# Five products a tile are added to their neighbours by an accumulating DMA from tile 8 on; GpSimd then adds four instead of seven, and TensorE sums twelve instead of fourteen

## The chip, the cores and the metric

The kernel runs on one core of a Trainium2 chip. It has five engines that run their own instruction queues and wait for each other by semaphores: TensorE (PE, with its weight loads as PEld), VectorE (DVE), ScalarE (ACT), GpSimd (POOL) and SyncE (SP), which here only issues DMAs. The metric is the time of one execution on the device, in microseconds; of several, the median is shown.

## The reference

A block of two halves on an image of 4 x 128 channels x 56 x 56. The first half is an involution: a 7 x 7 convolution whose kernel is computed for each pixel and each of 16 groups of channels. The second is a mixture of experts (8 experts, the best 2 for each token, hidden width 341).

```python
# conv half, on the layer-normed x
h = einsum('bchw,oc->bohw', xk, reduce_w) + reduce_b
kern = einsum('bchw,oc->bohw', h, span_w) + span_b      # 49 taps x 16 groups a pixel
out = (kern * patches).sum(axis=3)                      # sum over the 49 taps
x = x + out
# ffn half, on tokens
t = t + sum over the 2 chosen experts of gate * (silu(h1) * h3) @ w2.T
```

The change concerns only how `(kern * patches).sum` adds up its 49 products.

## The kernel before

The image is cut into 28 tiles of 8 rows (448 pixels). The 49 taps of a tile are taken as 24 pairs and one single, so 25 products (`TAPS`), numbered u = 0 to 24; a product of a pair is 128 x 896 floats, its two halves are two taps. One step of the program is one product: step S belongs to tile `p` and place `j` with `S = 25 p + j`, and each engine's program is written out as a loop over all steps (`for S in range(FIRST, END)`), so that each engine's order is fixed when the kernel is built.

For product g = 25 t + u:

- TensorE computes the pixel-wise kernel of the pair into `kern_ps[g % 2]` (`span_unit`, L586; two matmuls, one for the single). It waits until product g - 2 is done, since there are two such buffers.
- VectorE multiplies it with the shifted window of the normed image and writes `prod[g % 8]` (`unit`, L851; L839 for the single). The ring `prod` has `PRING = 8` slots, so before it writes, VectorE waits until the product eight before has been used (`consumer`).
- A product is then added up in one of three ways. **GpSimd** adds it to `acc_p` (`add`, L1084 for the first two, L1088 for the others). **VectorE** folds it into the next product: that product is made in `kern_ps` (L845) and the one before is added (L848). **TensorE** sums it into `acc_ps` by eight transposing matmuls with the identity (`sum_unit`, L601), the last of which for a tile takes `acc_p`.

Before, for tiles from `LATE = 8` on, GpSimd takes products 0, 3, 6, ..., 21 (seven additions), VectorE folds 10, 13, 16 and 19 into 11, 14, 17 and 20, and TensorE sums the other 13 and `acc_p`: 14 sums. The steps at which TensorE does its sums come from a small planner at the top of the kernel (`SUM_AT`): a sum is put two steps after its product or later, at the first step whose estimated load is under 1.3, and five steps after at the latest.

```python
while _left and at(_t, _left[0]) + 2 <= _S and (LOAD.get(_S, 0) < 1.3
        or min(at(_t, _left[0]) + 5, at(_t + 1, 2)) <= _S):
    SUM_AT.setdefault(_S, []).append((_t, _left.pop(0)))
```

When the tile is summed, VectorE adds the residual (`x1`, L1053), and ScalarE and GpSimd do its layer norm (`rsqrt`: L1074 and L1076 on GpSimd, for both norms). Tokens are routed to experts in groups of two tiles; GpSimd scatters their rows to DRAM by indirect DMAs (`scatter`, L1097), and the expert blocks of 512 tokens are computed on TensorE in between (L623 to L627, L536; `hid` on VectorE, L1024). Their results are added to the output by accumulating indirect DMAs (`add_rows`, L1109). Scatters stand at nine places of a late tile (`SCATTER_J`), token additions at nine (`ADD_J`). GpSimd's order within a step is: `rsqrt`, `add`, `scatter`, `add_rows`. After the last product the remaining expert blocks run as a tail.

Of the kernel before, what the change touches and what calls it, by code (L numbers as in the profile page):

```python
# [9 lines left out]
ALU = mybir.AluOpType  # L10
# [31 lines left out]
LATE = 8  # L42
BY_POOL = [tuple(range(0, 21, 2)) if t < LATE else tuple(range(0, 22, 3)) for t in range(TILES)]
BY_DVE = [() if t < LATE else (10, 13, 16, 19) for t in range(TILES)]
BY_PE = [tuple(u for u in range(TAPS) if u not in BY_POOL[t] + BY_DVE[t]) for t in range(TILES)]
ADD0 = [sum(len(BY_POOL[i]) - 1 for i in range(t)) for t in range(TILES + 1)]
PRING = 8
# [167 lines left out]
for _t in range(TILES):  # L215
    _S = at(_t, J_X1 + 1)
    _left = list(BY_PE[_t])
    while _left:
        while _left and at(_t, _left[0]) + 2 <= _S and (LOAD.get(_S, 0) < 1.3 or min(at(_t, _left[0]) + 5, at(_t + 1, 2)) <= _S):
            SUM_AT.setdefault(_S, []).append((_t, _left.pop(0)))  # L220
            LOAD[_S] = LOAD.get(_S, 0) + 1.04
        _S += 1
# [15 lines left out]
def build(nc, x, w_red, b_red, w_span, router, w13, w2, ident, lower, consts, tabs, ids, empty, out):  # L238
    with ExitStack() as ctx:  # L239
# [108 lines left out]
        s_prod = sem("s_prod")  # L348
        s_inner = sem("s_inner")
        s_sum = sem("s_sum")  # L350
        s_padd = sem("s_padd")
# [61 lines left out]
        def token_rows(dram, t):  # L413
            return dram[t * N:(t + 1) * N, :].rearrange("(q p) c -> p q c", p=SUB)

        def consumer(eng, t, u):

            if u in BY_POOL[t]:
                eng.wait_ge(s_padd, ADD0[t] + max(BY_POOL[t].index(u), 1))
            elif u in BY_DVE[t]:  # L420
                eng.wait_ge(s_prod, t * TAPS + u + 2)
            else:
                eng.wait_ge(s_sum, SUM_NO[(t, u)])
# [99 lines left out]
        def _(pe):  # L523
# [65 lines left out]
            def sum_unit(t, u):  # L589
                if u == BY_PE[t][0] and t:  # L590
                    pe.wait_ge(s_x1, t)
                if u < TAPS:
                    pe.wait_ge(s_prod, t * TAPS + u + 1)
                    src = prod[:, (t * TAPS + u) % PRING, :]
                else:
                    pe.wait_ge(s_padd, ADD0[t + 1])
                    src = acc_p[:]
# [463 lines left out]
        def _(pool):  # L1061
# [16 lines left out]
            def add(t, k):  # L1078
# [7 lines left out]
                else:  # L1086
                    pool.wait_ge(s_padd, ADD0[t] + k - 1)
                    g_.tensor_tensor(acc_p[:], acc_p[:], prod[:, (t * TAPS + u) % PRING, :], ALU.add).then_inc(s_padd, 1)  # L1088

            def scatter(t, q, k):  # L1090
                n = t * SUBS + q
# [21 lines left out]
            for S in range(FIRST, END):  # L1113
# [5 lines left out]
                if 0 <= p < TILES and j in BY_POOL[p][1:]:  # L1119
                    add(p, BY_POOL[p].index(j))  # L1120
                if S in SCATTER_AT:
                    scatter(*SCATTER_AT[S])
# [60 lines left out]
```

## Time and profile before

| | |
|---|---|
| median of 3 runs | 1502.02 us (1501.6 to 1506.93) |
| the profiled execution | 1498.94 us, span 1497.1 us |
| busy in the span | PE 1243.9 (83%), DVE 1122.8 (75%), POOL 1112.2 (74%), ACT 579.5 (39%) us |
| granted TensorE clock, mean | 0.95 |
| DMA | 120.40 MB, mean 80 GB/s |

Busy time of an engine counts its instructions and not its waiting. The average over the span mixes two stages: in the first, to about 1203 us, products are made; the tail after it has expert blocks only. A wait is put down to whatever came last before the waiting instruction began.

### The profile page before, as it was taken

To read this page: it belongs to the slowest core of one execution; us is meant where nothing else is said; L and a number is where in the kernel's file an instruction comes from. 1 tells how busy PE (TensorE), PEld (TensorE's weight loads), DVE (VectorE), ACT (ScalarE), POOL (GpSimd) and SP (SyncE) were. 2 spreads that over 40 slices of the span, in tenths; PEclk is the share of its full clock that TensorE was granted. 3 is DMA by queue.
4 is the path that set the end of the run, shared out by engine and by line. 5 is a ranking of instruction groups with operands and counts; after the bars stand their busy time and mean duration, and the time that the engine had idled before them with its cause. 6 is when DMAs were issued, how large, how long until landed. Compare 5 with 4: busy or idle time off the path is not lost. (4 is left out here: it accounts for less than half of the span.)

```text
span 1497.1 us, 23125 instructions
## 1 busy us (share of the span) xinstructions
PE 1243.9 (83%) x7667; PEld 1015.6 (68%) x7667; DVE 1122.8 (75%) x1663; ACT 579.5 (39%) x1960; POOL 1112.2 (74%) x788
## 2 busy tenths in 40 slices
PE   4898878788988989899899898899989887587771
PEld 2676767676766777677787777777778676465661
DVE  5998888988898998888889898888889943222220
ACT  4333333334443444444345343454434244133230
POOL 4787979784686887678788687877778875665665
PEclk9999898998999999999999999999999999899996
DMA  4111111112232242332324232243322445666652
GB/s 124 41 60 48 59 49 59 49 31 88 53 79 60 69 97 63 88 78 60 85 59 103 62 86 62 60 100 83 71 58 48 105 119 129 174 137 134 145 117 25
DMA packets 93346, 120.40 MB, mean 80 GB/s; under 512 B 11531, under 2 KB 72428, under 8 KB 93082
## 3 DMA queue, kind: packets, MB, share of 16 engines
q1 hardware_dynamic: 53802, 90.97, 20.0%
q0 software_dynamic: 39424, 27.96, 13.3%
q8 instruction: 61, 1.00, 0.3%
q14 instruction: 59, 0.48, 0.1%
HBM read 78.92 MB, written 42.65 MB: 81 GB/s over the span
## 5 line engine op out<-in xcount | busy, mean ns | idle before, releaser
L851 DVE TENSOR_TENSOR prod<-kern_ps,xn 128x896 f32<-128x896 f32 x592 | 627.9, 1082 | 65.7 <-PE kern_ps L586 63.2
L586 PE MATMUL kern_ps<-h_stack,span 98*128 98x448 f32 x1372 | 466.3, 426 | 112.7 <-DVE prod L851 72.1
L1088 POOL TENSOR_TENSOR acc_p<-acc_p,prod 128x896 f32<-128x896 f32 x192 | 435.9, 2270 | 74.1 <-DVE prod L851 69.4
L1109 POOL DMA_INDIRECT out<-y_tok,idx x224 | 351.6, 1570 | 137.4 <-issue 66.2
L601 PE MATMUL acc_ps<-ident_sb,prod 128*112 128x128 f32 x2864 | 388.4, 280 | 0.0
L601 PEld LDWEIGHTS acc_ps<-ident_sb,prod 128*112 128x112 f32 x2864 | 341.3, 137 | 37.9 <-DVE x L1053 7.8
L586 PEld LDWEIGHTS kern_ps<-h_stack,span 98*128 98x128 f32 x1372 | 227.1, 200 | 205.5 <-DVE prod L851 121.5
L1097 POOL DMA_INDIRECT xs<-rows_x,slots x224 | 219.0, 978 | 61.0 <-issue 41.3
L536 PEld LDWEIGHTS bank<-w2b,hid 114*128 114x128 f32 x1344 | 181.7, 202 | 50.7 <-DVE xf_lo L1046 26.0
L536 PE MATMUL bank<-w2b,hid 114*128 114x128 f32 x1344 | 190.1, 288 | 26.2 <-DVE xf_lo L1046 15.9
L780 ACT ACTIVATE silu<-h_ps 114x512 f32<-114x512 f32 x132 | 79.0, 598 | 235.0 <-PE h_ps L627 235.0
L1024 DVE TENSOR_TENSOR hid<-silu,h_ps 114x512 f32<-114x512 f32 x132 | 89.9, 681 | 97.9 <-ACT silu L780 68.8
L623 PE MATMUL h_ps<-xf_hi,wb 128*114 128x512 f32 x264 | 118.5, 449 | 15.3 <-ACT silu L780 13.6
L1084 POOL TENSOR_TENSOR acc_p<-prod 128x896 f32<-128x896 f32 x28 | 62.9, 2247 | 85.9 <-DVE prod L851 52.2
L685 ACT ACTIVATE y_tok<-bank,xb 128x128 f32<-128x128 f32 x224 | 64.1, 373 | 118.6 <-PE bank L536 98.1
L627 PE MATMUL h_ps<-xf_lo,wb 128*114 128x512 f32 x264 | 106.1, 402 | 0.0
L624 PE MATMUL h_ps<-xf_hi,wb 128*114 128x512 f32 x264 | 105.9, 401 | 0.0
L845 DVE TENSOR_TENSOR kern_ps<-kern_ps,xn 128x896 f32<-128x896 f32 x80 | 87.2, 1090 | 12.3 <-PE kern_ps L586 11.4
L848 DVE TENSOR_TENSOR prod<-kern_ps,prod 128x896 f32<-128x896 f32 x80 | 87.3, 1091 | 2.8
L1024 DVE TENSOR_TENSOR hid<-silu,kern_ps 114x512 f32<-114x512 f32 x36 | 24.7, 685 | 84.2 <-ACT silu L780 63.1
L1074 POOL TENSOR_TENSOR rstd_ln<-veps_ln,minus_half 112x4 f32<-112x4 f32 x56 | 67.0, 1196 | 15.0 <-ACT veps_ln L718 14.9
L755 ACT ACTIVATE rows_x<-x,shift_ln,rstd_ln 112x128 f32<-112x128 f32 x112 | 47.8, 485 | 56.4 <-POOL shift_ln L1076 56.3
(154 smaller groups left out, 1349.9 us busy)
## 6 DMA issues: line engine op xcount, KB each, us to landing
wb<-wexp SPq DMA_DIRECT2D x56, 684.0 KB, 5.4
xb<-xs SPq DMA_DIRECT2D x56, 264.0 KB, 3.0
w2b<-in_w SPq DMA_DIRECT2D x56, 171.0 KB
xt<-in_x SPq DMA_DIRECT2D x28, 224.0 KB, 3.4
out<-x SPq DMA_DIRECT2D x28, 224.0 KB, 2.6
wexp<-wb SPq DMA_DIRECT2D x8, 684.0 KB, 3.2
xs<-rows_x,slots POOLq DMA_INDIRECT x224, 2.3
out<-y_tok,idx POOLq DMA_INDIRECT x224
```

The lines of the kernel that those rows point to most:

```text
L536: i = mm(bank[:, k * C:(k + 1) * C], hid[:, (CPE * b + c) % HR, k * 128:(k + 1) * 128], w2b[:, b % 2, c, :], start=c == 0 and k == 0, stop ...
L586: last = mm(kern_ps[:, g % 2, i, 0:N], span[:, k * C:(k + 1) * C], h_stack[:, t % 2, :], start=True, stop=True)
L601: last = mm(acc_ps[0:SUB, k * C:(k + 1) * C], src[:, at_:at_ + SUB], ident_sb[:], is_transpose=True, start=u == BY_PE[t][0] and i == 0 and ...
L623: mm(ps, lo, xf_hi[:, b % 2, :], start=True, stop=False)
L624: mm(ps, hi, xf_hi[:, b % 2, :], start=False, stop=False)
L627: mm(ps, hi, xf_lo[:, b % 2, :], start=False, stop=True).then_inc(done, 1)
L848: v.tensor_tensor(dst.rearrange("p (i n) -> p i n", i=2), kern, prod[:, (g - 1) % PRING, :].rearrange("p (i n) -> p i n", i=2), ALU.add).t ...
L851: v.tensor_tensor(pair_rows(dst), kern.rearrange("p i (r w) -> p i r w", w=W), taps, ALU.mult).then_inc(s_prod, 1)
L1024: v.tensor_tensor(hid[:, n % HR, :], silu[:, n % 2, :], h_at(n, 1), ALU.mult).then_inc(s_hid, 1)
L1088: g_.tensor_tensor(acc_p[:], acc_p[:], prod[:, (t * TAPS + u) % PRING, :], ALU.add).then_inc(s_padd, 1)
L1097: g_.indirect_dma_start(out=xs, out_offset=bass.IndirectOffsetOnAxis(ap=slots[:, k, n:n + 1], axis=0), in_=rows_x[:, t % XN2RING, q, k, :] ...
L1109: g_.indirect_dma_start(out=out, out_offset=bass.IndirectOffsetOnAxis(ap=idx[:, b % XBRING, q:q + 1], axis=0), in_=y_tok[:, b % 2, q * C:( ...
```

## The change

From tile 8 on five products (1, 5, 11, 17 and 22, `BY_DMA`) are added to their right neighbours (2, 6, 12, 18 and 23) in SBUF by a DMA that accumulates, issued from GpSimd at the step of the neighbour, after GpSimd's own addition of that step and before its scatter. It waits for the neighbour's product. Four semaphores in turn (`MRING`) tell of the landings. GpSimd's own products are now 0, 4, 8, 15 and 21 (four additions), VectorE's folds are the same four, and TensorE sums eleven products and `acc_p`. A sum of a merged neighbour waits for the merge, and the planner puts it five steps after its product or later (`soonest`); `BY_PE` is sorted by the earliest step. VectorE, before it takes the slot of a merged product again, waits for that merge.

```diff
-BY_POOL = [tuple(range(0, 21, 2)) if t < LATE else tuple(range(0, 22, 3)) for t in range(TILES)]
+BY_POOL = [tuple(range(0, 21, 2)) if t < LATE else (0, 4, 8, 15, 21) for t in range(TILES)]
 BY_DVE = [() if t < LATE else (10, 13, 16, 19) for t in range(TILES)]
-BY_PE = [tuple(u for u in range(TAPS) if u not in BY_POOL[t] + BY_DVE[t]) for t in range(TILES)]
+
+BY_DMA = [() if t < LATE else (1, 5, 11, 17, 22) for t in range(TILES)]
+MERGE_NO = {(t, u): n for n, (t, u) in enumerate((t, u) for t in range(TILES) for u in BY_DMA[t])}
+MRING = 4
+
+def soonest(t, u):
+
+    return 5 if u - 1 in BY_DMA[t] else 2
+
+BY_PE = [tuple(sorted((u for u in range(TAPS) if u not in BY_POOL[t] + BY_DVE[t] + BY_DMA[t]),
+                      key=lambda u: u + soonest(t, u))) for t in range(TILES)]
...
-        while _left and at(_t, _left[0]) + 2 <= _S and (LOAD.get(_S, 0) < 1.3 or min(at(_t, _left[0]) + 5, at(_t + 1, 2)) <= _S):
+        while _left and at(_t, _left[0]) + soonest(_t, _left[0]) <= _S and (LOAD.get(_S, 0) < 1.3 or min(at(_t, _left[0]) + 5, at(_t + 1, 2)) <= _S):
...
+        def merged(eng, t, u):
+
+            n = MERGE_NO[(t, u)]
+            eng.wait_ge(s_merge[n % MRING], 16 * (n // MRING + 1))
+
         def consumer(eng, t, u):
 
             if u in BY_POOL[t]:
                 eng.wait_ge(s_padd, ADD0[t] + max(BY_POOL[t].index(u), 1))
+            elif u in BY_DMA[t]:
+                merged(eng, t, u)
...
                     pe.wait_ge(s_prod, t * TAPS + u + 1)
+                    if u - 1 in BY_DMA[t]:
+                        merged(pe, t, u - 1)
...
+            def merge(t, u):
+
+                n = MERGE_NO[(t, u)]
+                g = t * TAPS + u
+                pool.wait_ge(s_prod, g + 2)
+                if n >= MRING:
+                    pool.wait_ge(s_merge[n % MRING], 16 * (n // MRING))
+                g_.dma_start(prod[:, (g + 1) % PRING, :], prod[:, g % PRING, :], accum_op=ALU.add).then_inc(s_merge[n % MRING], 16)
...
+                if 0 <= p < TILES and j - 1 in BY_DMA[p]:
+                    merge(p, j - 1)
```

The program's order shows what stands where. On GpSimd, in tile 20 from step 4 to step 12, stood before (L1088 the additions of products 6, 9 and 12; L1097 a scatter, L1109 a token addition, L1074 and L1076 the second norm's `rsqrt`):

```order
L1097 DMA xs<-rows_x,slots 104960x132
L1109 DMA out<-y_tok,idx 13056x128
L1088 TENSOR_TENSOR acc_p<-acc_p,prod 128x896
L1097 DMA xs<-rows_x,slots 104960x132
L1109 DMA out<-y_tok,idx 13056x128
L1074 TENSOR_TENSOR rstd_ln<-veps_ln,minus_half 112x4
L1076 TENSOR_TENSOR shift_ln<-negmean_ln,rstd_ln 112x4
L1088 TENSOR_TENSOR acc_p<-acc_p,prod 128x896
L1097 DMA xs<-rows_x,slots 104960x132
L1109 DMA out<-y_tok,idx 13056x128
L1088 TENSOR_TENSOR acc_p<-acc_p,prod 128x896
```

and stands now, after the `rsqrt` of step 4 (L1106 and L1110 the additions of products 4 and 8, L1119 the merges of 5 and of 11, L1128 a scatter, L1140 a token addition):

```order
L1106 TENSOR_TENSOR acc_p<-prod 128x896
L1128 DMA xs<-rows_x,slots 104960x132
L1140 DMA out<-y_tok,idx 13056x128
L1119 DMA prod<-prod 128x896
L1128 DMA xs<-rows_x,slots 104960x132
L1110 TENSOR_TENSOR acc_p<-acc_p,prod 128x896
L1140 DMA out<-y_tok,idx 13056x128
L1096 TENSOR_TENSOR rstd_ln<-veps_ln,minus_half 112x4
L1098 TENSOR_TENSOR shift_ln<-negmean_ln,rstd_ln 112x4
L1128 DMA xs<-rows_x,slots 104960x132
L1140 DMA out<-y_tok,idx 13056x128
L1119 DMA prod<-prod 128x896
```

The merge of 5 into 6 stands behind the addition of product 4, a scatter and a token addition; five instructions stand between it and the merge of 11 into 12, besides the small ones of the norm.

On TensorE, in tile 20 from step 9 to step 12, stood before (L586 the matmuls of a product's kernel, L601 a sum, L623 to L627 an expert slot, L548 transposes of the next tile's input):

```order
L586 MATMUL kern_ps<-h_stack,span 128x448 x2
L601 MATMUL acc_ps<-ident_sb,prod 112x128 x8
L548 MATMUL bank<-ident_sb,xn_tok 128x112 x4
L586 MATMUL kern_ps<-h_stack,span 128x448 x2
L601 MATMUL acc_ps<-ident_sb,prod 112x128 x8
L623 MATMUL h_ps<-xf_hi,wb 114x512
L624 MATMUL h_ps<-xf_hi,wb 114x512
L627 MATMUL h_ps<-xf_lo,wb 114x512
L586 MATMUL kern_ps<-h_stack,span 128x448 x2
L601 MATMUL acc_ps<-ident_sb,prod 112x128 x8
L586 MATMUL kern_ps<-h_stack,span 128x448 x2
```

and stands now (L606, L623, L645 to L649 and L568 are the same in the new numbering):

```order
L606 MATMUL kern_ps<-h_stack,span 128x448 x2
L623 MATMUL acc_ps<-ident_sb,prod 112x128 x8
L568 MATMUL bank<-ident_sb,xn_tok 128x112 x4
L606 MATMUL kern_ps<-h_stack,span 128x448 x2
L645 MATMUL h_ps<-xf_hi,wb 114x512
L646 MATMUL h_ps<-xf_hi,wb 114x512
L649 MATMUL h_ps<-xf_lo,wb 114x512
L606 MATMUL kern_ps<-h_stack,span 128x448 x2
L623 MATMUL acc_ps<-ident_sb,prod 112x128 x8
L606 MATMUL kern_ps<-h_stack,span 128x448 x2
```

The sum of step 10 is gone, and the one of step 11 is now that of product 6, which waits for the merge of 5; the kernel matmuls of step 12 stand behind it.

## Rows read from the trace of the kernel before

**Rows 1.** Windows: busy us (count) by engine, clock, DMA share, GB/s.
```profile
347.00:1203.20 856.20, 766.61 (x4851) 638.00 (x4851) 749.87 (x1123) 359.37 (x1224) 668.86 (x481) 0.97 0.32 73
1203.20:1497.00 293.80, 200.55 (x1169) 156.18 (x1167) 77.67 (x172) 93.51 (x253) 181.48 (x128) 0.92 0.56 125
```

**Rows 2.** Chain of waits in the tail: start us, us, what.
```profile
1355.68 1.55 POOL out L1109
...
1357.53 3.95 DMA out<-y_tok,idx
...
1362.45 1.55 POOL out L1109
```

**Rows 3.** Waits, 347 to 1203 us: total us, times, longest.
```profile
PE kern_ps L586 <- DVE prod L851: 38.8, 53, 2.7
...
PE kern_ps L586 <- DVE prod L848: 33.5, 43, 1.6
DVE prod L851 <- PE kern_ps L586: 32.9, 58, 1.5
...
DVE kern_ps L845 <- PE kern_ps L586: 11.0, 14, 1.3
DVE hid L1024 <- PE h_ps L627: 10.7, 17, 2.0
...
DVE kern_ps L908 <- PE kern_ps L586: 8.2, 9, 1.8
```

**Rows 4.** TensorE by line, 346 to 1203 us: busy us, mean ns | idle.
```profile
L601 PE MATMUL acc_ps<-ident_sb,prod 128*112 128x128 f32 x1891 | 251.2, 276 | 0.0
```

**Rows 5.** GpSimd by line and shape, 346 to 1203 us.
```profile
L1088 POOL TENSOR_TENSOR acc_p<-acc_p,prod 128x896 f32<-128x896 f32 x114 | 270.7, 2375 | 61.7 <-DVE prod L851 61.5
L1109 POOL DMA_INDIRECT out<-y_tok,idx x124 | 196.1, 1582 | 44.8 <-issue 34.6 <-ACT y_tok L685 6.8 <-DMA out<-y_tok,idx 2.1
L1097 POOL DMA_INDIRECT xs<-rows_x,slots x150 | 146.0, 973 | 34.9 <-issue 19.9 <-POOL acc_p L1088 12.0 <-ACT rows_x L740 2.3
L1074 POOL TENSOR_TENSOR rstd_ln<-veps_ln,minus_half 112x4 f32<-112x4 f32 x37 | 46.6, 1259 | 8.7 <-ACT veps_ln L718 8.7
```

**Rows 6.** The page: DMA queues (packets, MB, share); issues with landing.
```profile
q1 hardware_dynamic: 53802, 90.97, 20.0%
q0 software_dynamic: 39424, 27.96, 13.3%
...
wb<-wexp SPq DMA_DIRECT2D x56, 684.0 KB, 5.4
...
xs<-rows_x,slots POOLq DMA_INDIRECT x224, 2.3
```

**Rows 7.** Timeline of tile 20, VectorE: start us, us, instruction.
```profile
851.52 1.09 DVE L851 TENSOR_TENSOR prod<-kern_ps,xn 128x896 f32<-128x896 f32 x1 [0.56 <-PE kern_ps L586]
...
853.12 4.22 DVE L851 TENSOR_TENSOR prod<-kern_ps,xn 128x896 f32<-128x896 f32 x4
...
864.05 1.08 DVE L851 TENSOR_TENSOR prod<-kern_ps,xn 128x896 f32<-128x896 f32 x1
```

**Rows 8.** Timeline of tile 20, TensorE.
```profile
861.29 0.57 PE L586 MATMUL kern_ps<-h_stack,span 98*128 98x448 f32 x2
861.71 1.04 PE L601 MATMUL acc_ps<-ident_sb,prod 128*112 128x128 f32 x8
...
870.81 0.65 PE L586 MATMUL kern_ps<-h_stack,span 98*128 98x448 f32 x2
```

**Rows 9.** Timeline of tile 20, GpSimd.
```profile
852.51 1.04 POOL L1074 TENSOR_TENSOR rstd_ln<-veps_ln,minus_half 112x4 f32<-112x4 f32 x1 [0.59 <-ACT veps_ln L718]
853.63 0.20 POOL L1076 TENSOR_TENSOR shift_ln<-negmean_ln,rstd_ln 112x4 f32<-112x4 f32 x1
...
868.47 2.70 POOL L1088 TENSOR_TENSOR acc_p<-acc_p,prod 128x896 f32<-128x896 f32 x1
```

More of the change, by code:

```diff
@@ L349, in build @@
         s_inner = sem("s_inner")
+        s_merge = [sem(f"s_merge{i}") for i in range(MRING)]
         s_sum = sem("s_sum")
```

## The prediction

> **What bounds the kernel now.** I read the windows first. [rows 1] splits the span: from 347 to 1203 us run 19 of the 20 changed tiles, and from 1203 to 1497 us comes a tail in which no product is made any more. In the first stretch TensorE is busy 767 of 856 us, VectorE 750, GpSimd 669, and the 16 DMA engines 0.32 of the time. Three engines are nearly full and the transfers are not. The chain of waits comes next: in the tail it is made of the token additions alone, GpSimd's issues and their landings [rows 2]. No product, no sum and no addition to `acc_p` stands in it, so the change cannot touch the tail; what the first stretch gains or loses shifts the tail one for one.
>
> Within the stretch the waits [rows 3] say how TensorE and VectorE hold each other. `kern_ps` has two buffers, so TensorE may be one product ahead and no more. VectorE waits for TensorE's `kern_ps` 32.9 us before plain products, 11.0 before folded ones and 8.2 before routing steps that stand in front of a product, and 10.7 us for the hidden layer: 62.8 us, or 3.3 us a tile. TensorE in turn waits 38.8 + 33.5 = 72.3 us for VectorE's products, 3.8 us a tile. So neither is the bound alone: work taken from TensorE helps only in those steps where VectorE was the one waiting, and a new wait of TensorE hurts at once only where TensorE had no time to spare.
>
> **What is removed.** Two sums a tile leave TensorE. The sums of products are 1891 matmuls in 251.2 us [rows 4], eight to a sum, hence 1.06 us a sum; 2 x 1.06 x 20 tiles = 43 us of TensorE. Both ends of what that is worth: nothing if VectorE sets the pace in those steps, all 43 us if TensorE does. The waits are split about evenly between the two (62.8 against 72.3 us), so I take half, 21 us. The second order fence shows one of the places: step 10 loses its sum, in a run of steps in which TensorE did not idle.
>
> GpSimd loses three additions a tile, each 270.7 / 114 = 2.37 us [rows 5]: 7.1 us a tile. It gets five issues of an accumulating DMA. No such issue from one tile to another stands in the trace. The nearest rows are the scatter (112 rows, 0.97 us) and the token addition, which accumulates (128 rows, 1.58 us) [rows 5]; I take 1.3 us, between them, and keep both ends. 5 x (1.3 + 0.16 between instructions) = 7.3 us. So GpSimd stays as full as it was (669 of 856 us), and this is the point on which the rest turns: the merges stand in a queue that is not early.
>
> VectorE's own work does not change: the same 25 products and the same four folds. Where it takes a slot of `prod` again it now waits for a merge instead of an addition or a sum. That wait comes eight products after the source, about 10 us after the merge may begin, and I cost it at nothing as long as a merge lands within that; with the late ends below it would begin to bind at step 13 or 19, but behind the same merge that TensorE already waits for, so it isn't added.
>
> **What a merge takes.** It moves 128 x 3584 B = 459 KB. From its issue, a scatter of 56 KB lands in 2.3 us (a median), a load of 684 KB of weights in 5.4 us [rows 6]. Over the whole profile the hardware queue q1 moved 90.97 MB in 20.0% of 16 x 1497 us, 19.0 GB/s an engine; the software queue q0, in which the accumulating transfers run, 27.96 MB in 13.3%, 8.8 GB/s [rows 6]. A merge gives each of 16 engines 28.7 KB: 1.5 us at the one rate and 3.3 us at the other. Low end of landing: 2.3 + 1.5 = 3.8 us. High end: the token addition of the tail, issued at 1355.68 and landed at 1357.53 + 3.95 = 1361.48 [rows 2], takes 5.8 us from its issue for only 64 KB, in DRAM; with 3.3 - 0.4 us more of data 8.7 us. A merge reads and writes SBUF like the scatter's source and needs no reading of DRAM, so I stay nearer to the scatter: 2.3 + 0.3 for a longer issue + 2.1 of data more than the scatter's + 0.5 for sharing the engines with the loads = 5.2 us. (100 merges x 2.3 us of every engine add 0.26 to the DMA share of 0.32: no saturation.)
>
> The Trainium skill ("DMA: Bandwidth & Descriptors", the section on the anatomy of one DMA from GpSimd) gives about 2.0 us plus the bytes at 436 GB/s; an estimate from that page is 3.1 us for a merge. The trace agrees for the small scatter and not for the 684 KB load, which takes 5.4 us where the page's line gives 3.6. The skill's "Collectives: The Full Stack" (the bandwidth ceiling: the fold count) says that an adding transfer has two sources to read and so runs at half the rate of a copy; q0 at 8.8 against q1 at 19.0 GB/s fits that, though small rows are in it too.
>
> **When a merge is asked for.** I follow tile 20, in its own times. The planner puts the sum that needs the merge of 5 into 6 on TensorE in step 11, and that of 11 into 12 in step 17. Before, product 4 ends at 852.61, product 6 near 855.2 (the second of the four that start at 853.12), product 12 at 865.13 [rows 7]. TensorE has finished the kernel matmuls of step 11 at 861.86 and of step 17 at 871.46 [rows 8]; there it would stop.
>
> GpSimd's queue (the first order fence) before the merge of 5: the little products for `rstd` and `shift`, which end at 853.83 [rows 9], then the first addition (2.37), a scatter (0.98 + 0.16) and a token addition (1.58 + 0.30): 859.2. Product 6 has been ready for 4.0 us by then. It lands at 859.2 + 5.2 = 864.4, that is 2.5 us after TensorE stands at it. Then, in the queue: the merge's issue 1.46, scatter 1.14, addition 2.37, token addition 1.88, `rstd` and `shift` 1.55, scatter 1.14, token addition 1.88: the merge of 11 goes out at 870.6 and lands at 875.8, 4.3 us after TensorE came to it before the change, of which 2.5 have been lost already. That GpSimd is this late is no fiction of mine: the trace of before has its addition of product 12 start at 868.47 [rows 9], 3.3 us after that product.
>
> Tile 20 is a full one. There were 124 token additions and 150 scatters in 19 tiles [rows 5], 6.5 and 7.9 a tile where nine places for each are planned, so 0.28 and 0.12 of the places are empty. Up to step 17 three of each stand in the queue: 3 x (0.28 x 1.88 + 0.12 x 1.14) = 2.0 us less on average. 4.3 - 2.0 = 2.3 us a tile; some of it falls into time in which TensorE waited for VectorE anyway (folded products stand at steps 11, 14, 17 and 20), so I take 1.9. The merges of 17, 22 and 1 are issued when GpSimd has caught up, and their products leave five steps of about 1.8 us: 9 us less the step or so by which TensorE runs ahead, against 5.2: nothing. Sum: 1.9 x 20 = 38 us lost.
>
> What stands behind the waiting sum on TensorE is the kernel matmul of step 12 (second order fence), and VectorE's product 12 waits for that: the stall reaches the pace with little in between.
>
> **The sum.** -21 + 38 = +17 us. The profiled execution took 1498.9 us with a span of 1497.1; the median of the runs shown is 1502.0, 3.1 above it, and I set the difference on the median: 1519 us.
>
> **The rivals.**
> First, the merges land soon enough, and the kernel is faster. Place: TensorE at the sums of steps 11 and 17. With the low ends, landing 3.8 and issue 0.97, the queue reaches the merge of 11 at 870.3 and it lands at 874.1, 2.6 us after TensorE, less 2.0 for empty places: 0.6 us x 20 = 12 us, against 21 of relief: 1493 us; with more of the 43 us given back, down to 1480. The point from which it decides: a loss of 21 us is 1.05 us a tile, 0.85 less than mine, so a landing below about 4.3 us from the issue makes the kernel faster. For it: the scatter's 2.3 us, and half-idle DMA engines. Against: 4.0 us of lateness on GpSimd before the transfer even begins. By the Trainium skill's line for one DMA, above, the landing would be under this point.
>
> Second, no change. TensorE idles 3.8 us a tile for VectorE [rows 3]; if the merges' stalls fall into that, and what is saved at TensorE goes there too, the stretch stays at VectorE's pace: 1502 us. For it: VectorE is busy 750 of 856 us and its work is untouched. Against: VectorE has 3.3 us a tile of waiting for TensorE.
>
> Third, the transfer is slow, near its high end. With issue 1.58 and landing 8.7, 870.9 + 8.7 - 871.5 - 2.0 = 6.1 us a tile, 122 us, less 21: 1603 us. VectorE's wait for a slot would join in. Half-way, at 7 us, it is 3.7 x 20 - 21 = 53: 1555 us. For it: the token additions' 5.8 us. Against: these go to DRAM.
>
> **How the numbers follow.** The forecast, a few microseconds lost to late merges net of the relief, has 0.42; the first rival 0.28; the second 0.20; the third 0.10. About 0.5%, 7.5 us, is what a measurement of this kernel can tell from no change (the three runs lie between 1501.6 and 1506.9). Faster: the first rival, 0.28; same: 0.20; slower: 0.42 + 0.10 = 0.52. The forecast's own range is 1510 to 1540. Eight in ten takes in most of the first rival and the third to a landing of about 7 us: 1484 to 1560.
>
> **What would show it.** Right: the issue-to-landing of the merges near 5 us; the merge of 5 issued some 3 to 4 us after product 6; a new row among the waits, TensorE's sums for the merge, of 1 us and more a piece at steps 11 and 17; VectorE's waits for `kern_ps` grown there and shrunk in the steps around the tile's start; GpSimd as busy as before; the tail 294 us long. The forecast is wrong if the landing is 4 us or less, if an issue on GpSimd costs well under 1 us (its queue would then never be late), or if the rows of waits for the merge are short and the changed tiles take less than the 45.1 us they take now (856.2 / 19).

## The result and the profile after

The changed kernel takes 1555.2 us (median of 4 runs, 1549.1 to 1560.4) against 1501.8 (4 runs): ratio 1.0345, 95% interval 1.0319 to 1.037, so 3.5% slower, 53 us. The profiled execution took 1556.3 us with a span of 1554.5, which is 57.4 above the span of before. One run of the kernel before, in the last group of runs below, took 6467 us and is left out of its median.

Where the time went is answered first by the windows. Here are, of the changed kernel, the same 19 tiles as in [rows 1] and the tail after them, in the same columns (us, busy us and count of TensorE, its weight load, VectorE, ScalarE, GpSimd, then the granted clock, the DMA share and GB/s):

```profile
347.50:1256.60 909.10, 758.54 (x4558) 620.59 (x4558) 746.77 (x1124) 357.90 (x1224) 643.62 (x519) 0.94 0.56 118
1256.60:1554.00 297.40, 203.24 (x1162) 159.21 (x1160) 77.51 (x170) 94.32 (x253) 182.21 (x129) 0.89 0.58 124
```

The stretch of 19 tiles takes 909.1 us where it took 856.2: 52.9 of the 57.4 us, or 2.8 us a tile. The tail has grown by 4, the start by half a microsecond. No engine has become fuller: TensorE is busy 759 us (767 before), VectorE 747 (750), GpSimd 644 (669). All stand longer. Only the DMA share is much higher, 0.56 for 0.32.

The waits of the same stretch say what they stand for (total us, times, longest); compare [rows 3]:

```profile
PE acc_ps L623 <- DMA prod<-prod: 67.2, 39, 6.0
PE kern_ps L606 <- DVE prod L870: 30.1, 29, 1.7
PE kern_ps L606 <- DVE prod L873: 25.3, 48, 1.3
...
PE bank L574 <- ACT rows_x L777: 1.6, 3, 0.7
DVE prod L873 <- PE kern_ps L606: 42.6, 48, 5.3
DVE xf_lo L1068 <- ACT xf_hi L699: 19.6, 17, 5.2
DVE ge L1000 <- PE kern_ps L606: 17.9, 4, 6.5
DVE hid L1046 <- PE h_ps L649: 17.5, 15, 2.7
...
DVE kern_ps L930 <- PE kern_ps L606: 8.4, 8, 1.8
DVE kern_ps L867 <- PE kern_ps L606: 5.8, 14, 1.3
```

The first row is new: TensorE stands at a sum until a merge has landed, 67 us. Its waits for VectorE shrank only from 72.3 to 55.4 us. VectorE waits more for TensorE: the longest piece before a plain product is 5.3 us where it was 1.5, the mark of a TensorE that has stopped. Over the whole span the page has the same wait at 68.8 us, in the group that answers to [rows 4], and the merge's issues stand further down:

```profile
L623 PE MATMUL acc_ps<-ident_sb,prod 128*112 128x128 f32 x2544 | 359.4, 287 | 73.8 <-DMA prod<-prod 68.8
...
L1119 POOL DMA_DIRECT2D prod<-prod x100 | 114.2, 1142 | 101.9 <-DVE prod L873 101.0
```

GpSimd by line in the stretch answers to [rows 5]:

```profile
L1140 POOL DMA_INDIRECT out<-y_tok,idx x124 | 197.3, 1591 | 34.8 <-issue 34.6 <-ACT rows_x L762 0.2
L1128 POOL DMA_INDIRECT xs<-rows_x,slots x150 | 149.9, 1000 | 40.9 <-issue 33.6 <-ACT rows_x L762 5.7 <-POOL acc_p L1106 1.0
L1110 POOL TENSOR_TENSOR acc_p<-acc_p,prod 128x896 f32<-128x896 f32 x57 | 123.7, 2169 | 66.9 <-DVE prod L873 66.6
L1119 POOL DMA_DIRECT2D prod<-prod x95 | 109.4, 1152 | 97.8 <-DVE prod L873 96.9 <-DVE prod L861 0.8
```

95 issues in 19 tiles, 1.15 us each on average. GpSimd also idles 97 us in front of them, waiting for the product, 46 times of 95: about half of the merges are not late at all when they are issued. The page's queues answer to [rows 6]:

```profile
q0 software_dynamic: 53824, 73.84, 28.9%
q1 hardware_dynamic: 53802, 90.97, 19.7%
```

The merges brought q0 45.9 MB in 14,400 packets; its share rose from 13.3% of 1497 us to 28.9% of 1554.5.

Now the walk through tile 20, which answers to [rows 7 to 9]. GpSimd's timeline (start us, us, instruction, idle before it) around the merge of 5:

```profile
881.46 2.10 POOL L1106 TENSOR_TENSOR acc_p<-prod 128x896 f32<-128x896 f32 x1
883.73 1.03 POOL L1128 DMA_INDIRECT xs<-rows_x,slots  x1 [0.16 <-POOL acc_p L1106]
885.06 1.61 POOL L1140 DMA_INDIRECT out<-y_tok,idx  x1 [0.30 <-issue]
886.08 1.57 POOL L1119 DMA_DIRECT2D prod<-prod  x1
...
896.69 1.54 POOL L1119 DMA_DIRECT2D prod<-prod  x1
```

VectorE's products 5 to 7 of the tile:

```profile
880.78 3.17 DVE L873 TENSOR_TENSOR prod<-kern_ps,xn 128x896 f32<-128x896 f32 x3
```

and TensorE at the sums of steps 11 and 17:

```profile
887.45 0.57 PE L606 MATMUL kern_ps<-h_stack,span 98*128 98x448 f32 x2
891.16 1.06 PE L623 MATMUL acc_ps<-ident_sb,prod 128*112 128x128 f32 x8 [3.14 <-DMA prod<-prod]
...
901.86 1.06 PE L623 MATMUL acc_ps<-ident_sb,prod 128*112 128x128 f32 x8 [0.39 <-DMA prod<-prod]
```

Product 6, the second of the three, is ready at 882.9. GpSimd comes to the merge at 886.1, 3.2 us later. TensorE is done with the kernel matmuls at 888.0 and starts the sum at 891.2: 5.1 us from the issue to the sum, 3.1 us stood. The merge of 11 is issued at 896.69 and its sum starts at 901.86, 5.2 us later, with 0.4 us stood. This tile follows the prediction's walk closely at step 11. The odd tile before it does not. SyncE's and GpSimd's issues in tile 19:

```profile
829.07 0.34 SPq L505 DMA_DIRECT2D xb<-xs  x1
829.46 0.42 SPq L530 DMA_DIRECT2D out<-x  x1
829.93 0.48 SPq L532 DMA_DIRECT2D xt<-in_x  x1
...
831.16 1.56 POOL L1119 DMA_DIRECT2D prod<-prod  x1
831.39 0.22 SPq L514 DMA_DIRECT2D wb<-wexp  x1
```

and its sum on TensorE:

```profile
841.44 1.93 PE L623 MATMUL acc_ps<-ident_sb,prod 128*112 128x128 f32 x8 [4.88 <-DMA prod<-prod]
```

Here the merge is asked for promptly, but 10.3 us pass from the issue to the sum, beside 264 + 224 + 224 + 684 KB of loads and stores, and TensorE stands 4.9 us. What I counted from the timeline over all 20 tiles, by merge: at that of 5 TensorE stands 46.1 us (in every tile), at that of 22 14.0, at that of 11 7.8, at that of 1 5.9, at that of 17 nothing: together the 73.8 us that the page shows as idle before these matmuls, of which it puts 68.8 on the merge.

The 46.1 us at the merge of 5 have two causes, and they go by the tile's number. In the ten even tiles (21.8 us) the merge goes out 1.2 to 4.5 us after product 6 and its sum starts 4.5 to 5.3 us after the issue. In the ten odd tiles (24.3 us) it goes out 0.3 to 1.6 us after the product, so GpSimd is hardly late, but 5.9 to 10.3 us pass from the issue to the sum. Those ten part again by the loads beside them. In tiles 11, 15, 19, 23 and 27 SyncE issues a load of expert weights (684 KB) within 3 us of the merge, and it takes 8.1 to 10.3 us; in the other five no such load is that near, and it takes 5.9 to 7.1 us.

### The profile page after: what moved, and what is told of

Read it like the earlier page. It is cut to its first block and busy times, and to the rows that moved or that the text cites. A ratio compares the mean times of both kernels' runs of the same rounds, so it can differ in the third digit from the quotient of the medians.

```text
span 1554.5 us, 22661 instructions
## 1 busy us (share of the span) xinstructions
PE 1237.2 (80%) x7347; PEld 998.3 (64%) x7347; DVE 1118.3 (72%) x1663; ACT 578.9 (37%) x1960; POOL 1086.5 (70%) x828
## 3 DMA queue, kind: packets, MB, share of 16 engines
q0 software_dynamic: 53824, 73.84, 28.9%
q1 hardware_dynamic: 53802, 90.97, 19.7%
## 5 line engine op out<-in xcount | busy, mean ns | idle before, releaser
L606 PE MATMUL kern_ps<-h_stack,span 98*128 98x448 f32 x1372 | 468.3, 427 | 97.7 <-DVE prod L873 60.4
L1140 POOL DMA_INDIRECT out<-y_tok,idx x224 | 352.7, 1575 | 130.8 <-issue 62.7
L623 PE MATMUL acc_ps<-ident_sb,prod 128*112 128x128 f32 x2544 | 359.4, 287 | 73.8 <-DMA prod<-prod 68.8
L623 PEld LDWEIGHTS acc_ps<-ident_sb,prod 128*112 128x112 f32 x2544 | 311.5, 141 | 120.0 <-issue 45.2
L606 PEld LDWEIGHTS kern_ps<-h_stack,span 98*128 98x128 f32 x1372 | 228.8, 201 | 189.4 <-DVE prod L873 102.2
L1110 POOL TENSOR_TENSOR acc_p<-acc_p,prod 128x896 f32<-128x896 f32 x132 | 282.5, 2140 | 81.1 <-DVE prod L873 76.5
L1128 POOL DMA_INDIRECT xs<-rows_x,slots x224 | 223.4, 997 | 67.2 <-issue 55.7
L556 PEld LDWEIGHTS bank<-w2b,hid 114*128 114x128 f32 x1344 | 185.1, 205 | 50.0 <-DVE xf_lo L1068 24.1
L556 PE MATMUL bank<-w2b,hid 114*128 114x128 f32 x1344 | 193.5, 291 | 25.5 <-DVE xf_lo L1068 13.6
L1119 POOL DMA_DIRECT2D prod<-prod x100 | 114.2, 1142 | 101.9 <-DVE prod L873 101.0
L645 PE MATMUL h_ps<-xf_hi,wb 128*114 128x512 f32 x264 | 119.4, 452 | 14.5 <-ACT silu L802 13.4
L649 PE MATMUL h_ps<-xf_lo,wb 128*114 128x512 f32 x264 | 107.3, 406 | 0.0
L1106 POOL TENSOR_TENSOR acc_p<-prod 128x896 f32<-128x896 f32 x28 | 59.0, 2106 | 50.0 <-PE acc_ps L623 32.4
L1096 POOL TENSOR_TENSOR rstd_ln<-veps_ln,minus_half 112x4 f32<-112x4 f32 x56 | 74.5, 1330 | 25.4 <-ACT veps_ln L740 25.3
```

Of the source, the lines that this page charges most:

```text
L556: i = mm(bank[:, k * C:(k + 1) * C], hid[:, (CPE * b + c) % HR, k * 128:(k + 1) * 128], w2b[:, b % 2, c, :], start=c == 0 and k == 0, stop ...
L606: last = mm(kern_ps[:, g % 2, i, 0:N], span[:, k * C:(k + 1) * C], h_stack[:, t % 2, :], start=True, stop=True)
L623: last = mm(acc_ps[0:SUB, k * C:(k + 1) * C], src[:, at_:at_ + SUB], ident_sb[:], is_transpose=True, start=u == BY_PE[t][0] and i == 0 and ...
L645: mm(ps, lo, xf_hi[:, b % 2, :], start=True, stop=False)
L649: mm(ps, hi, xf_lo[:, b % 2, :], start=False, stop=True).then_inc(done, 1)
L1119: g_.dma_start(prod[:, (g + 1) % PRING, :], prod[:, g % PRING, :], accum_op=ALU.add).then_inc(s_merge[n % MRING], 16)
```

## The experiments

Every ratio is to the kernel before, run on the same chip in the same group; its median was 1503.2, 1503.1 and 1503.7 us in the three groups. Experiments 1, 2, 5 and 6 are of the first group, 3, 7, 8 and 9 of the second, 4, 10, 11 and 12 of the third. Waits quoted are of the stretch from 347 to 1257 us.

**1. No merges at all.** GpSimd issues none, nothing waits for one, five products a tile are left out of the output. The rest keeps its order.

```diff
-                merged(eng, t, u)
+                pass
...
-                    if u - 1 in BY_DMA[t]:
-                        merged(pe, t, u - 1)
...
-                if 0 <= p < TILES and j - 1 in BY_DMA[p]:
-                    merge(p, j - 1)
```

> The changed kernel's order with the five merges a tile left out altogether, issue, transfer and waits; products 1, 5, 11, 17 and 22 of the late tiles are then missing from the output. It shows what the lighter TensorE and GpSimd are worth by themselves. Theory A (the whole loss is TensorE standing at sums whose merge has not landed, and the relief is what I took, about 21 us): 1475 to 1485 us, near 1480. Rival B (nothing is relieved, VectorE sets the pace): 1500 us or a little more. Rival C (the planner's moved sums are themselves bad for the pace): above 1505 us even without merges.

Measured: 1480.4 us, ratio 0.986 (0.9836 to 0.9884). Two sums and three additions fewer a tile are worth 23 us together. That is near the prediction's 21, but the 21 were for TensorE's two sums alone: the three additions had been set against the five issues. How the 23 us divide between the two engines no run separates, so the agreement may be partly luck.

**2. Merges issued, nobody waits for them.** They add a product onto itself (the same bytes), and TensorE's wait is gone.

```diff
-                    if u - 1 in BY_DMA[t]:
-                        merged(pe, t, u - 1)
...
-                g_.dma_start(prod[:, (g + 1) % PRING, :], prod[:, g % PRING, :], accum_op=ALU.add)...
+                g_.dma_start(prod[:, g % PRING, :], prod[:, g % PRING, :], accum_op=ALU.add)...
```

> All five merges a tile are issued at their places and move the same bytes, but each adds its product to itself and TensorE's sums do not wait for it (only the reuse of the slot does); the five products are missing from the sums. Theory A (the wait at TensorE): within 5 us of the kernel without merges, 1475 to 1490 us, and no wait of TensorE on a transfer. Rival D (the traffic itself is the cost: it slows the loads of weights and tokens, or GpSimd's queue with five issues of 1.0 to 1.5 us is what holds the pace): 1520 us or more, most of the 53 us still there.

Measured: 1500.1 us (10 runs), ratio 0.9977 (0.9964 to 0.999). My own number was missed: issuing and moving the merges alone costs 19.7 us, and takes back nearly the whole relief. The wait for them is then worth 1555.2 - 1500.1 = 55 us (of two groups of runs, in which the kernel before lies 1.4 us apart). Where the 20 us may sit, the waits of this kernel show:

```profile
ACT rows_x L775 <- POOL shift_ln L1096: 89.3, 19, 7.0
PE bank L574 <- ACT rows_x L775: 35.0, 12, 5.0
```

ScalarE waits for GpSimd's `shift`, the end of the second norm's small products, and TensorE for the rows that ScalarE normalises with it. The same two waits in the kernel before, and then in experiment 1:

```profile
ACT rows_x L755 <- POOL shift_ln L1076: 28.4, 16, 3.8
PE bank L554 <- ACT rows_x L755: 3.9, 2, 3.5
```

```profile
ACT rows_x L775 <- POOL shift_ln L1096: 60.4, 19, 5.6
PE bank L574 <- ACT rows_x L775: 13.5, 6, 3.3
```

So the norm was late before any merge was issued. The first two order fences show what may have done it: the change moved an addition (now of product 8, in step 8) from behind the norm's small products of step 9, where that of product 9 stood, to ahead of them. The issue of the merge of 5 then comes on top. ScalarE's wait goes from 28 to 60 us with the additions moved and to 89 with the issues.

**3. The same with half the bytes** separates the issue from the traffic.

```diff
-                g_.dma_start(prod[:, g % PRING, :], prod[:, g % PRING, :], accum_op=ALU.add)...
+                g_.dma_start(prod[:, g % PRING, 0:N], prod[:, g % PRING, 0:N], accum_op=ALU.add)...
```

> As the kernel in which nobody waits for the merges (1500 us), with half of the bytes of each, 1792 B a row; same number of issues and of packets. The 20 us between it and the kernel without merges are either transfers in the way of other transfers (theory D: then about half of them go, 1490 us) or five issues a tile of 1.0 to 1.5 us on GpSimd, behind which the second norm's rsqrt stands and for that TensorE (theory F: 1497 to 1502 us, no change, and TensorE still waits about 35 us for ScalarE's normed rows).

Measured: 1499.8 us (10 runs), ratio 0.9978 (0.9964 to 0.9993), the same as with all bytes. The software queue's share fell from 29.9% to 22.5% of the engines, nearly half of what the merges had added, and nothing was won. So the 20 us are not the bytes. They are what stayed the same, the five issues in GpSimd's queue or the number of packets; experiment 4 bears on which.

**4. The norm first.** Experiment 2, with the addition of product 8 and the token addition of step 8 put behind the second norm's small products:

```diff
+                if LATE <= p < TILES and j == 9:
+                    add(p, 2)
...
+                hold = LATE <= p < TILES and j == 8
```

> As the kernel in which nobody waits for the merges (1500 us; 20 us above the one without merges), but GpSimd does the second norm's rsqrt before its addition of product 8 (and the token addition of step 8) instead of after them. Theory F (the five issues make GpSimd late for that rsqrt, ScalarE then norms the rows late, and TensorE waits 35 us for them): most of that wait goes, 1483 to 1490 us. Rival J (the 20 us sit elsewhere: in VectorE's waits for GpSimd's additions, in TensorE's other waits): 1497 to 1502 us.

Measured: 1487.5 us, ratio 0.989 (0.9866 to 0.9914). And the same two waits:

```profile
ACT rows_x L775 <- POOL shift_ln L1096: 36.8, 19, 3.4
PE bank L574 <- ACT rows_x L775: 4.5, 4, 2.8
```

The norm's lateness was worth 13 us of this kernel. GpSimd's work is the same here; only its order differs. Not all of the 13 need belong to the issues: the edit also takes away what the moved addition does, and TensorE's wait for the rows falls by 30.5 us, to under the 13.5 of experiment 1. The control, this order with no merges at all, was not run.

**5. Four merges, without that of 5**, the whole kernel otherwise (TensorE has a sum more).

```diff
-BY_DMA = [() if t < LATE else (1, 5, 11, 17, 22) for t in range(TILES)]
+BY_DMA = [() if t < LATE else (1, 11, 17, 22) for t in range(TILES)]
```

> A whole kernel: only 1, 11, 17 and 22 are merged; TensorE sums 5 and 6 itself, so thirteen sums a tile instead of twelve. The merge of 5 accounts for 46 of the 74 us that TensorE waits for merges. Theory A: those 46 us go, a sum of 1.06 us comes back in 20 tiles at half its weight (10 us): about 1519 us (1510 to 1528). Rival E (any merge hurts alike, the 53 us are spread over the five): 1545 us. If the wait only moves to the next merge, between the two.

Measured: 1535.1 us, ratio 1.0204 (1.0155 to 1.0253). Expected by my count was 1519. The wait for merges fell to this row:

```profile
PE acc_ps L623 <- DMA prod<-prod: 28.7, 18, 4.1
```

The merge of 5 is the dearest, but 20 us are won and not 46: with it gone, the wait at that of 22 grew from 14 to 21 us.

**6. The merge of 5 earlier**, ahead of the addition of product 4.

```diff
+                if LATE <= p < TILES and j == 6:
+                    add(p, 1)
```

> A whole kernel: GpSimd issues the merge of 5 before its addition of product 4 instead of after it; all else as in the changed kernel. Theory A1 (the merge of 5 is late because it is issued late): in the even tiles it is issued 2.1 to 4.5 us after its product and lands 5.1 us later, in the odd tiles 0.3 to 1.6 us after it and lands 6 to 10 us later beside a load of weights. An addition is 2.1 us, so the even tiles should win about 2 us each and the odd ones little: 10 x 2 + 10 x 0.5 = 25 us, 1530 us. Rival A2 (the landing alone matters): no change, 1550 to 1556 us.

Measured: 1558.6 us, ratio 1.0378 (1.0345 to 1.041). Neither expectation held. In the even tiles the merge did come sooner, by some 1.6 us; in the odd ones it had been prompt already. TensorE's wait for that of 5 fell from 46 to 5.4 us in both, and mostly because TensorE itself came later (8.7 us after product 6, median, for 5.8). It was held by a wait that I had overlooked:

```profile
DVE prod L873 <- POOL acc_p L1106: 49.2, 18, 5.5
PE acc_ps L623 <- DMA prod<-prod: 28.0, 23, 3.7
```

The first addition also frees the slot of product 0, which VectorE needs for product 8. The run says nothing against the mechanism; it says that this addition has a date of its own.

**7. Scatter and token addition of steps 4 and 5 held** until the merge of 5 is issued.

```diff
+                hold = LATE <= p < TILES and j in (4, 5)
+                for S_ in (S - 2, S - 1, S) if LATE <= p < TILES and j == 6 else () if hold else (S,):
```

> A whole kernel: in late tiles the scatter of step 4 and the token addition of step 5 are held back on GpSimd until the merge of 5 is issued in step 6; the additions of products stay where they are, so no slot of prod is freed later. Putting the addition of product 4 behind that merge had taken 40 us of TensorE's wait for the merge of 5 away and given 49 us of VectorE waiting for the slot of product 0 instead. Theory A1 (half of the lateness is GpSimd's queue): the merge of 5 goes out up to 3.0 us sooner in the even tiles, where TensorE waited 22 us for it, and hardly sooner in the odd ones: 15 to 20 us won, 1535 to 1540 us. Rival A2 (the landing beside the loads sets it in all tiles, since an earlier merge meets the step's other transfers): less than 8 us won.

Measured: 1552.2 us, ratio 1.0323 (1.0301 to 1.0345). That is 3 us won, the rival's number, but not for the rival's reason. Two rows show the exchange:

```profile
PE acc_ps L623 <- DMA prod<-prod: 50.6, 33, 4.2
PE bank L574 <- ACT rows_x L777: 22.4, 10, 4.3
```

The merge waits fell by 17 us (at that of 5 from 46 to 17 us, by 19 in even tiles and by 10 in odd ones), and the transposes of the normalised rows, 1.6 us late in the changed kernel, are 22.4 us late: what I had pushed back now stands between the merge and the norm.

**8. Less traffic beside the merge of 5.** Half of each block's expert weights is loaded (the other half is left out), and the store of `x` and the load of the next input stand at step 14 instead of step 6.

```diff
-                                 wexp[bass.ds(w * C, C), :]).then_inc(s_wb[b % 2], 16)
+                                 wexp[bass.ds(w * C, C), 0:2 * HALL]).then_inc(s_wb[b % 2], 16)
...
-                if j == J_X1 + 1 and 1 <= p <= TILES:
+                if j == 14 and 1 <= p <= TILES:
```

> The changed kernel with less traffic beside the merge of 5: of each block's 684 KB of weights only the first half is loaded (the other half keeps what is in the buffer, so the expert outputs are wrong), and the x1 store and xt load of step 6 are issued at step 14. Theory G (in the odd tiles the merge of 5 lands 6 to 10 us after its issue because 0.9 to 1.4 MB of other loads are in flight): it lands in 5 to 6 us there, the 25 us of waits in odd tiles fall to about 8, those for 1 and 22 by half (10 us): 1525 to 1532 us. Rival H (the landing does not depend on the loads): 1550 us or more.

Measured: 1517.6 us (6 runs), ratio 1.0094 (1.0064 to 1.0125): 38 us less than the changed kernel, more than I expected. The same merge of tile 19 as above, GpSimd and TensorE:

```profile
827.90 1.56 POOL L1119 DMA_DIRECT2D prod<-prod  x1
```

```profile
834.34 1.05 PE L623 MATMUL acc_ps<-ident_sb,prod 128*112 128x128 f32 x8 [1.07 <-DMA prod<-prod]
```

6.4 us for 10.3. Over the ten odd tiles the last packet of the merge of 5 ends 5.2 us after the issue, median, where it was 7.2; in the even ones it stays at 4.6. Not every odd tile gained: from issue to sum it is still 8.9 us in tile 11 (10.3) and 7.0 in tile 21 (6.7). The edit took away less than it says, too: by the trace the store of `x`, in most cases with the load, still goes out within about 3 us of the merge of 5 in half of the 20 tiles. In the odd tiles TensorE's wait at the merge of 5 fell from about 24 to 9.5 us in all; in the even ones it did not (21.8 to 25.3). TensorE's whole wait for merges is then 39.4 us, 28 less than in the stretch of the changed kernel. The remaining 10 us I did not separate: VectorE also waits less for the experts' rows (`xf_lo` 12.8 us for 19.6), and both halves of the edit act together.

**9. The sum that needs the merge of 5 two steps later** (step 13).

```diff
-    return 5 if u - 1 in BY_DMA[t] else 2
+    return (7 if u == 6 else 5) if u - 1 in BY_DMA[t] else 2
```

> A whole kernel: TensorE's sum of product 6 stands seven steps after its product, in step 13, instead of five. Transfers, issues and lateness stay. Theory A (each us of TensorE's stand at the merge of 5 costs a us of pace): two steps are 3.2 us, so of the 46 us about 8 remain: 1515 to 1520 us. Rival I (the stall only turns into VectorE waiting for the slot of product 6, which product 14 takes): 1540 us or more, with VectorE idle before product 14.

Measured: 1531.7 us, ratio 1.0176 (1.0141 to 1.0212). The wait at the merge of 5 went from 46 to 1.4 us, but 23 us were won. Two rows show what came instead:

```profile
PE acc_ps L623 <- DMA prod<-prod: 35.8, 26, 3.6
PE bank L574 <- ACT rows_x L777: 18.1, 8, 4.0
```

The wait at the merge of 11 rose from 7.8 to 12.6 us, and the norm is late again, which fits that a TensorE standing at step 11 had given GpSimd time to catch up.

**10. Both: the late sum, and the norm first** as in experiment 4.

> A whole kernel: all five merges, TensorE's sum of product 6 in step 13 (1532 us by itself, with the wait for the merge of 5 gone but 18 us of waits for the normed rows instead) and GpSimd's second rsqrt before its addition of product 8. Theories A and F together: the 18 us go, 1512 to 1518 us. If VectorE's pace is held by the merges of 1, 11 and 22 alone, 1525 to 1532 us.

Measured: 1553.7 us, ratio 1.0352 (1.032 to 1.0385), a plain miss of some 38 us.

```profile
PE acc_ps L623 <- DMA prod<-prod: 62.0, 30, 5.6
```

The wait for the normalised rows is gone, but what I put behind the norm stands in front of the merge of 11: TensorE waits 38.3 us at that one. GpSimd has three customers between steps 4 and 13 (merge of 5, norm, merge of 11), and whichever is served first makes another late.

**11. Three merges** (1, 11, 17) and 14 sums.

```diff
+BY_DMA = [() if t < LATE else (1, 11, 17) for t in range(TILES)]
```

> A whole kernel: only 1, 11 and 17 are merged, the three for which TensorE waited 5.9, 7.8 and 0 us; TensorE does 14 sums as before the change, GpSimd four additions and three issues instead of seven additions. Without the merge of 5 alone it was 1535 us. Theory A (the waits for 5 and 22 are the loss): 1535 less the 21 us that TensorE waited there for the merge of 22, plus a sum at half its weight (10 us), and fewer collisions: 1515 to 1525 us. Theory F (GpSimd's queue is what was filled up): three issues instead of five and no merge ahead of the second norm's rsqrt: 1500 to 1510 us. Rival (any use of the accumulating DMA costs in proportion to its number): 1503 + 3/5 x 53 = 1535 us.

Measured: 1522.5 us, ratio 1.0119 (1.0097 to 1.0142).

```profile
PE acc_ps L623 <- DMA prod<-prod: 16.3, 11, 3.1
```

This is the number of theory A. Three merges still cost 19 us, with 16.3 us of waits for them, most at that of 1 (13.0 us in 20 tiles for 5.9 in the changed kernel).

**12. One merge** (of 1), with the additions of the kernel before.

```diff
+BY_POOL = [tuple(range(0, 21, 2)) if t < LATE else tuple(range(0, 22, 3)) for t in range(TILES)]
...
+BY_DMA = [() if t < LATE else (1,) for t in range(TILES)]
```

> A whole kernel, a try at a faster one: the kernel before with one merge, of 1 into 2; GpSimd keeps its seven additions and TensorE has 13 sums. Theory A: one sum less is half of 21 us at half weight... worked out: the relief of two sums and three additions was 23 us, of which one sum may be 8 to 10; the merge of 1 costs about 6 us of waits and one issue (1 us x 20 on GpSimd, hidden where it is not late): 1497 to 1502 us, near 1500. Theory F: GpSimd, kept at seven additions and given an issue more, is late for its additions and the norm: 1505 to 1510 us.

Measured: 1517.8 us (6 runs), ratio 1.0101 (1.0082 to 1.012). Neither expectation held, the nearest being 1505 to 1510 us: even one merge a tile makes the kernel 1% slower.

```profile
PE acc_ps L623 <- DMA prod<-prod: 12.2, 9, 3.0
```

GpSimd kept its seven additions, so the issue came on top; the wait explains 12 us of the loss of 14, but TensorE also had a sum less to do. Where that relief went is open.

No kernel with all its products in the output beats the one before.

## Why the prediction came out as it did

The sign was right, and so was the place: TensorE stands at the sum of product 6 in all 20 tiles. The reason given, that GpSimd's queue issues the merge of 5 late, holds for the even tiles, with 21.8 of the 46 us; in the odd ones the transfer is slow. The size was off, 17 us forecast and 53 measured. Step by step:

| term | forecast | measured | by |
|---|---|---|---|
| relief of TensorE (forecast), of TensorE and GpSimd (measured) | -21 | -23 | experiment 1 |
| five issues in GpSimd's queue | 0 (set against the three additions) | +20 | 2 against 1 |
| TensorE standing at merges | +38 | +55 | changed kernel against 2 |
| sum | +17 | +52 | |

Free of that mismatch is the sum of the first two rows: -21 forecast, -3 measured (1500.1 against 1503.2 in one group). Two steps failed, and about equally: by 18 us here and by 17 at the standing.

**The first step that failed** is the sentence "GpSimd stays as full as it was", from which I let the swap of three additions for five issues cost nothing but the lateness of the merges themselves. The arithmetic was nearly right: 1.15 us an issue for the 1.3 taken, and GpSimd is busy 644 us for 669. But the queue has a third customer, the small products of the second norm, and I never asked when TensorE needs those rows. Nor did I ask where the remaining additions stand: one had moved from behind that norm to ahead of it, and TensorE's wait for the rows was 13.5 us for 3.9 already without merges. Experiments 2 to 4 show the cost: same bytes or half, +20 us; the norm moved ahead, 13 us come back, an unknown part of them the moved addition's. The other 7 have no row of their own. In the changed kernel this term hardly shows: its wait for `rows_x` is 1.6 us only, since TensorE already stands at step 11 and the norm catches up meanwhile. Experiment 7 takes most of that stall away and 9 nearly all, and the wait is back, 22 and 18 us. So the split of the table depends on the order in which the terms are taken away; the sum does not.

**The second step that failed** is the term for standing at merges, 38 us for the measured 55. It was sized too low in two places.

- The landing. 5.2 us was right in the even tiles (5.1 in tile 20). In the odd tiles such loads stand beside the merge of 5, on top of the store of `x` and the load of the next input that every tile has near it, and 5.9 to 10.3 us pass from the issue to the sum. I had reckoned the share of the engines over the whole stretch (0.32 + 0.26) and called it no saturation; what is in flight in the few microseconds of the transfer is what the landing follows. Experiment 8 supports it from the other side, with 5.2 for 7.2 us in the odd tiles, in a kernel that loads half of the weights.
- "The merges of 17, 22 and 1 cost nothing": that of 17 does, 22 and 1 cost 20 us of standing. I gave the five steps 9 us, less a step. TensorE comes to the sum 5.5 us (median) after the product at 22 and 5.8 at 5; at 1 it is 7.6, and there it is again the landing that is slow, up to 7.7 us.

**The walk of the merge of 11** went the other way: 4.3 us cumulative forecast at step 17, of which 1.8 beyond the first stall; measured 7.8 us in 20 tiles, 0.4 a tile. In tile 20 GpSimd was as late as forecast, 2.7 us after product 12 (the walk gives 3.0 when the first stall is counted in), and the landing was 5.2. TensorE was what differed: it comes to the sum 7.5 us after that product, where it came 6.3 after it before.

**Smaller points.** Some stalls cost more than their length: the sum at 841.44 took 1.93 us for the usual 1.06. So did four more of the 20 at the merge of 5 (tiles 10, 11, 23 and 27) and one at that of 22; the one in tile 20, after 3.1 us of standing, did not. The two windows of the changed kernel before and after the end of the stall in tile 19, in the columns of [rows 1], show the granted clock fall after TensorE had stood:

```profile
838.00:841.00 3.00, 0.00 (x0) 0.00 (x0) 0.82 (x1) 0.36 (x1) 0.62 (x1) 1.00 0.47 108
841.00:843.00 2.00, 1.56 (x8) 1.59 (x9) 0.00 (x0) 0.00 (x0) 0.00 (x0) 0.51 0.01 2
```

0.51 is the lower of the clock's two levels, 1.2 GHz. Over the stretch the clock is 0.94 for 0.97, and a sum's matmul takes 285 ns for 276: 9 x 1596 = 14 us of TensorE in all. Experiment 2, in which nobody stands at a merge, has 281 ns, so 6 us at most of these go with the standing. The slot of `prod` was, as forecast, no wait of VectorE's. The tail kept its length to 4 us. GpSimd did not stay as busy: 0.71 of the stretch for 0.78.

Of the rivals, the first (merges land in time) needed a landing under 4.3 us: from issue to sum none at which TensorE stood was. The second (no change) fell with experiment 1, in which the relief is worth 23 us at once. The third, a slow transfer, holds for odd tiles alone; its half-way figure of 1555 us is the measured time by luck, from other parts: half of the tiles at 6 to 10 us, and the 20 us of the issues.

## What to carry to other kernels

When work moves to a queue that several engines wait for, list every customer of that queue with its own date, not the queue's fill: here five issues of 1 us a tile cost 20 us in all, much of it because small products behind them are on another engine's path, and an addition moved ahead of those probably acted the same way. Before pricing an exchange, compare the two orders and not only the two sums of busy time. Size a transfer's landing by what is in flight in those microseconds, not by the mean share. And when one wait is taken away, look for what it had been giving time to; experiments 5, 6, 7, 9 and 10 each traded one wait for the next.

## What the runs showed of the hardware

- An accumulating DMA of 128 rows of 3584 B from SBUF to SBUF takes GpSimd 0.96 us to issue (median; 0.89 to 1.59). The row of all hundred in the changed kernel (minimum, median, maximum in ns):

```profile
L1119 POOL DMA_DIRECT2D prod<-prod x100: 886/963/1594, 314.8 to 1256.3; - x100
```

  It is near 1.55 us in 29 of the 100, each time right behind a token addition, which accumulates too (886.08 above). There the two records overlap, here by 0.6 us (885.06 + 1.61 = 886.67), so the longer time isn't shown to be the issue's own.
- A 3584 B row of a merge takes one DMA engine 301 ns (median), 11.9 GB/s, where the whole hardware queue ran at 19.0 in the kernel before. From issue to a sum that stood for it, it is 4.4 us at best (merge of 22), 5.1 behind a token addition (0.6 of it the overlap above), and up to 10.3 us beside 1.4 MB of other transfers.
- GpSimd's addition of 128x896 took 2.37 us before and 2.17 after, with VectorE busy 0.88 and 0.82 of the stretch. That the two hinder each other would explain it; it wasn't tested.
